# Attention with a windowed softmax and routed experts on one core: the order of the turned norm, queries, keys, values and exponentials between the two units of a tile

## The chip, the cores and the metric

One NeuronCore of one Trainium2 chip. The metric is the device time of one execution in microseconds; the program runs on one core.

## The reference

`x` is 8 sequences of 1024 positions of 128 features, in float32. The block computes

```python
x = x + attn(layernorm(x), Wq, Wk, Wv, Wo)      # 16 heads of 8, window of the last 64 positions
x = x + ffn(layernorm(x), w_router, w1, w2, bias)  # 8 experts, top 2 with a capacity, GELU
```

In `attn` the scores `q.k * 8**-0.5` of each position with the 64 positions up to itself go through a softmax and weigh the values; the heads, side by side, are multiplied by `Wo`. In `ffn` each position is sent to its two best experts (as far as they have room) and the results are added, weighted by the gates.

## The kernel before, in words

The attention part works in slots, one for each tile of 128 positions: 8 slots a sequence (t = 0 to 7), 64 in all, `slot(b, t)`. Each engine has its own `slot`, a list written out by hand, run in that order; semaphores tie the lists together. The chip's engines are TensorE (PE), VectorE (DVE), ScalarE (ACT), GpSimd (POOL) and SyncE (SP, which issues transfers).

A slot has two units, u = 2g and 2g + 1 for slot number g, for two groups of heads; each has its own two banks of `sT_ps`. For one unit:

- TensorE fills the banks with the window's mask and the scores (`fill`, lines 1108 to 1118). This is done a slot ahead.
- VectorE takes maxima over parts of them, turned (`part_max`, line 687, writes `kmax`).
- TensorE turns these again (`maxima_T`, line 1127, into `tail_ps` for first units and `o_ps` for second units).
- VectorE reduces them and prepares the shift (`shifts`, lines 693 to 701, writes `moving`).
- TensorE adds the shift to the scores (`shifted`, line 1135).
- ScalarE takes the exponential (`exps`, line 520, writes `probsT`).
- TensorE weighs the values with it (`weighted`, line 1143, into `u_ps`).

Once both units of a tile are weighted, ScalarE copies `u_ps` (`weighted_out`, line 525), TensorE turns it (`weighted_T`, line 1152, into `o_ps`), VectorE divides by the sums (`normalise`, lines 709 and 713), TensorE folds it (`context_T`, line 1158), ScalarE copies it (line 529), TensorE multiplies by `Wo` (`project`, line 1163), and VectorE adds `x` (`residual`, line 722). These steps run in the two following slots.

For each pair of tiles (n, numbered through all sequences) there is the preparation: ScalarE makes the normed rows (`normed`, line 473), TensorE turns them (`normed_T`, line 1086), ScalarE copies them (line 488); TensorE makes queries and keys (`query_key`, lines 1092 and 1093), ScalarE copies queries into a block form, four instructions (line 495), and keys, two (line 499); TensorE makes values (`values`, line 1098), ScalarE copies them in four instructions (line 510). All of it goes through one bank, `proj_ps`. The turned norm comes in even slots, queries and keys in odd ones, both in the first half of the slot (ahead of `shifted(2g + 1)`); values of the pair that begins in the next slot come in the second half of odd slots.

Other work sits at certain slots from the second sequence on: the second norm's rows of the sequence before are made by ScalarE in slot 4 (`normed_again`, line 482), turned by TensorE in slots 4 and 5 (line 1169, in `o_ps`) and copied by ScalarE in slot 5 (line 533); the router's matmuls stand in slots 5 and 6 (line 1193); VectorE's statistics, norm steps and routing are spread over all slots (`gap`, `small`). GpSimd sends routed rows and adds the bias, at counts of `s_scoresT`. After the attention part the experts run. VectorE's list is, for each slot: part maxima of unit 2g + 1, small work, `residual`, `shifts(2g + 1)`, part maxima of unit 2g + 2, small work, `normalise`, `shifts(2g + 2)`.

TensorE's list is that of the second `slot` printed below, ScalarE's the first; the lines of the diff are in them. A semaphore is waited for by count, as here in ScalarE's copy of queries (a pair's buffer is free when the scores of the pair before last are made):

```python
act.wait_ge(s_qk, n + 1)
if n >= 2:
    act.wait_ge(s_fill, 4 * n - 4)
```

Of the kernel before, what the change touches and what calls it, by code (L numbers as in the profile page):

```python
# [22 lines left out]
PAIRS = TILES // 2  # L23
# [25 lines left out]
def moe_block_kernel(nc, x, wq, wk, wv, wo, w_router, w1, w2, bias, out):  # L49
    ctx = ExitStack()  # L50
    with ctx:
# [410 lines left out]
        def _(act):  # L462
# [27 lines left out]
            def query_key(n, p, bank=proj_ps):  # L490
                act.wait_ge(s_qk, n + 1)
                if n >= 2:
                    act.wait_ge(s_fill, 4 * n - 4)
                for h in range(HQ):
                    nc.scalar.activation(qbd[:, p % 2, :, :, h, :].rearrange("p s b q -> p (s b) q"),  # L495
                                         bank[:, 0:2 * P].rearrange("p (c q) -> p c q", q=BLK), ACT.Copy,
                                         scale=quadmask[:, h:h + 1])
                for gp in range(2):
                    last = nc.scalar.activation(kT[:, gp, BLK + p * 2 * P:BLK + (p + 1) * 2 * P],
                                                bank[:, 2 * P:4 * P], ACT.Copy, scale=evenodd[:, gp:gp + 1])  # L500
                last.then_inc(s_k_sb, 1)
# [52 lines left out]
            def slot(b, t, first=False, last=False):  # L554
# [4 lines left out]
                if t == 7 and not first:  # L559
                    gate_exps(b - 1)  # L560
                if not (first and t == 0):
                    weighted_out(g - 1)
                if t % 2 == 0 and (t < 4 or not last):
                    normed_T(b * PAIRS + (t + 4) // 2, (t + 4) // 2 % PAIRS)
                if t % 2 == 1 and (t < 5 or not last):
                    query_key(b * PAIRS + (t + 3) // 2, (t + 3) // 2 % PAIRS)
# [4 lines left out]
                exps(g, 1)  # L571
                if t == 4 and not first:
                    normed_again(b, 1)
                if t % 2 == 1 and (t < 7 or not last):
                    values(b * PAIRS + (t + 1) // 2, (t + 1) // 2 % PAIRS)
                if t == 0 or t in (4, 6) and not last:
                    normed(b * PAIRS + (t + 6) // 2)
                if t == 3 and not last:
                    normed(b * PAIRS + 4)
# [6 lines left out]
            query_key(0, 0)  # L586
# [5 lines left out]
            query_key(1, 1, u_ps)  # L592
# [487 lines left out]
        def _(pe):  # L1080
# [126 lines left out]
            def slot(b, t, first=False, last=False):  # L1207
# [4 lines left out]
                shifted(2 * g)  # L1212
                if done:
                    pe.wait_ge(s_exp, 2 * g)
                    weighted((t - 1) % TILES, 1)
# [7 lines left out]
                if t % 2 == 1 and (t < 5 or not last):  # L1223
                    query_key(b * PAIRS + (t + 3) // 2, (t + 3) // 2 % PAIRS)
                if t % 2 == 0 and (t < 4 or not last):
                    n = b * PAIRS + (t + 4) // 2
                    pe.wait_ge(s_v_sb, n - 1)
                    pe.wait_ge(s_k_sb, n)
                    normed_T(n, (t + 4) // 2 % PAIRS)
# [3 lines left out]
                maxima_T(2 * g + 1)  # L1233
                pe.wait_ge(s_exp, 2 * g + 1)
                if ahead:
                    if t % 2 == 1:
                        pe.wait_ge(s_k_sb, b * PAIRS + (t + 1) // 2 + 1)
                    fill((t + 1) % TILES, 0)
                if t == 5 and not first:
# [19 lines left out]
                if t % 2 == 1 and (t < 7 or not last):  # L1259
                    n = b * PAIRS + (t + 1) // 2  # L1260
                    if t < 5 or not last:
                        pe.wait_ge(s_k_sb, n + 2)
                    values(n, (t + 1) // 2 % PAIRS)
# [143 lines left out]
```

## Time and profile before

| | |
|---|---|
| median of 3 runs | 861.02 us (860.0 to 861.64) |
| the profiled execution | 864.88 us, span 863.0 us |
| PE busy (matmuls) | 760.3 us, 88% of the span |
| PE weight loads | 544.6 us, 63% |
| DVE busy | 519.1 us, 60% |
| ACT busy | 451.1 us, 52% |
| POOL busy | 357.1 us, 41% |
| the exponentials (L520) | 128 of 1035 ns, 132.4 us |
| the part maxima (L687) | 128 of 1246 ns, 159.5 us |

The span is one profiled execution on the core. Busy times are sums over it; a matmul's end is modelled and matmuls are pipelined, so a busy PE isn't at its peak, and weight loads (PEld) overlap matmuls. In a row of the timeline the first number is the start in us from the span's start, the second the length; several like instructions are merged into one row (x8); in brackets stands how long the engine had been idle before and what ended that. L687 is line 687 of the kernel. The attention part fills some 555 us of the span, the experts the rest.

### The profile page before, as it was taken

The numbers are of one execution on the slowest core, as the hardware profiler recorded it, in microseconds if no ns is written. First come the engines' busy times: TensorE is split into PE (matmuls) and PEld (weight loads), VectorE is DVE, ScalarE is ACT, GpSimd is POOL, SyncE is SP. The second block draws the span as 40 slices with busy tenths as digits, with TensorE's granted clock in tenths as the row PEclk, the third lists the DMA queues.
The fourth block names the chain that finished last, engine by engine and source line by source line (L and its number), as shares of the span: only waits on it lengthen the run. The fifth ranks groups of instructions, "written<-read, shape, count | busy, mean of one in ns | idle before, by whom it ended". The sixth has DMA issues, their size and how long they took to land. (4 is left out here: it accounts for less than half of the span.)

```text
span 863.0 us, 19198 instructions
## 1 busy us (share of the span) xinstructions
PE 760.3 (88%) x7469; PEld 544.6 (63%) x7469; DVE 519.1 (60%) x1623; ACT 451.1 (52%) x923; POOL 357.1 (41%) x318
## 2 busy tenths in 40 slices
PE   7999999999999999999999998427999889889983
PEld 3556666666566566566666555314988778778872
DVE  7888888988888888887887887610222212211210
ACT  5576685585585585585586664202444334334421
POOL 3000000032232222322322343562877877877877
PEclk9999999999999999999999999557999999999997
DMA  4942000010110010010010011113364554554533
GB/s 137 387 160 62 8 15 8 34 33 25 50 33 21 31 47 30 22 56 30 21 57 30 21 66 40 67 51 117 32 111 59 93 101 58 96 97 59 87 31 33
DMA packets 50132, 54.21 MB, mean 63 GB/s; under 512 B 6018, under 2 KB 39449, under 8 KB 49025
## 3 DMA queue, kind: packets, MB, share of 16 engines
q0 software_dynamic: 22528, 17.22, 14.0%
q1 hardware_dynamic: 27520, 35.86, 12.6%
q8 instruction: 56, 0.92, 0.4%
q14 instruction: 28, 0.22, 0.1%
HBM read 17.70 MB, written 31.59 MB: 57 GB/s over the span
## 5 line engine op out<-in xcount | busy, mean ns | idle before, releaser
L445 POOL DMA_INDIRECT out<-y_sb,xg x128 | 199.2, 1556 | 71.1 <-issue 55.0
L363 POOL DMA_INDIRECT slots_dram<-send_rows,slot_id x112 | 110.3, 985 | 229.4 <-PE sT_ps L1135 163.1
L520 ACT ACTIVATE probsT<-sT_ps 128x1024 f32<-128x1024 f32 x128 | 132.4, 1035 | 60.2 <-PE sT_ps L1135 58.7
L687 DVE TRANSPOSE_TENSOR_REDUCE kmax<-sT_ps 128x32 f32<-128x1024 f32 x128 | 159.5, 1246 | 6.2 <-PE sT_ps L1118 5.7
L619 ACT ACTIVATE hT<-sT_ps 128x512 f32<-128x512 f32 x128 | 76.6, 599 | 154.7 <-PE sT_ps L1347 139.1
L1118 PE MATMUL sT_ps<-qbd,kT 64*128 64x256 f32 x1024 | 133.2, 380 | 0.0
L1347 PE MATMUL sT_ps<-xT_hl,w_hl 128*128 128x512 f32 x384 | 105.1, 426 | 24.8 <-DVE xT_hl L1045 18.5
L1055 DVE TENSOR_TENSOR y_sb<-o_ps,xg 128x256 f32<-128x256 f32 x32 | 13.6, 425 | 188.3 <-DMA out<-y_sb,xg 106.2
L1118 PEld LDWEIGHTS sT_ps<-qbd,kT 64*128 64x128 f32 x1024 | 98.6, 191 | 9.8
L1347 PEld LDWEIGHTS sT_ps<-xT_hl,w_hl 128*128 128x128 f32 x384 | 75.9, 204 | 43.9 <-DVE xT_hl L1045 19.1
L380 POOL TENSOR_TENSOR xbias<-x_sb,bias_sb 128x256 f32<-128x256 f32 x32 | 23.5, 734 | 192.8 <-PE sT_ps L1135 192.8
L1143 PE MATMUL u_ps<-probsT,v_sb 128*32 128x128 f32 x2048 | 82.9, 280 | 0.0
L1135 PE MATMUL sT_ps<-moving,ones 64*128 64x512 bf16 x256 | 49.9, 386 | 21.4 <-DVE moving L701 17.9
L1143 PEld LDWEIGHTS u_ps<-probsT,v_sb 128*32 128x32 f32 x2048 | 48.3, 109 | 29.6 <-issue 29.4
L1359 PE MATMUL o_ps<-w_sb,hT 128*128 128x128 f32 x512 | 62.7, 275 | 0.0
L1359 PE MATMUL proj_ps<-w_sb,hT 128*128 128x128 f32 x512 | 62.4, 275 | 0.0
L1359 PEld LDWEIGHTS o_ps<-w_sb,hT 128*128 128x128 f32 x512 | 59.8, 192 | 0.3 <-ACT hT L619 0.2
L1359 PEld LDWEIGHTS proj_ps<-w_sb,hT 128*128 128x128 f32 x512 | 59.7, 192 | 0.0
L701 DVE TENSOR_TENSOR moving<-negmax_hl,blocks 128x512 bf16<-128x512 bf16 x128 | 54.4, 425 | 4.4
L529 ACT COPY ctxT<-tail_ps 128x128 f32<-128x128 f32 x64 | 17.0, 266 | 72.6 <-PE tail_ps L1158 72.4
L495 ACT ACTIVATE qbd<-proj_ps,quadmask 128x256 f32<-128x256 f32 x124 | 48.7, 475 | 11.3 <-PE proj_ps L1093 9.8
L510 ACT ACTIVATE v_sb<-proj_ps 128x256 f32<-128x256 f32 (+1 forms) x124 | 37.2, 324 | 32.7 <-PE proj_ps L1098 31.9
(171 smaller groups left out, 1124.7 us busy)
## 6 DMA issues: line engine op xcount, KB each, us to landing
slots_dram<-empty_rows SPq DMA_DIRECT2D x8, 1096.0 KB, 16.7
xg<-slots_dram SPq DMA_DIRECT2D x32, 274.0 KB
out<-xbias SPq DMA_DIRECT2D x32, 128.0 KB
w_sb<-in_L_ffn_w SPq DMA_DIRECT2D x16, 256.0 KB
send_rows<-rows_sb SPq DMA_DIRECT2D x7, 548.0 KB, 3.2
out<-y_sb,xg POOLq DMA_INDIRECT x128
slots_dram<-send_rows,slot_id POOLq DMA_INDIRECT x112
out<-empty_rows SPq DMA_DIRECT2D x1, 1024.0 KB, 24.4
```

The costliest lines, as they stand in the source:

```text
L363: pool.indirect_dma_start(out=slots_dram, out_offset=bass.IndirectOffsetOnAxis(ap=slots[:, k, j:j + 1].bitcast(U32), axis=0), in_=rows[:, ...
L445: pool.indirect_dma_start(out=out, out_offset=bass.IndirectOffsetOnAxis(ap=xg[:, r, 4 * c + k, ROW - 1:ROW].bitcast(U32), axis=0), in_=y_s ...
L495: nc.scalar.activation(qbd[:, p % 2, :, :, h, :].rearrange("p s b q -> p (s b) q"), bank[:, 0:2 * P].rearrange("p (c q) -> p c q", q=BLK), ...
L520: nc.scalar.activation(probsT[:, gp].rearrange("p b k h q -> p (b k h q)"), sT_ps[:, gp].rearrange("p b c -> p (b c)"), ACT.Exp).then_inc( ...
L619: nc.scalar.activation(hT[:, c % 2, f, :], hidden_ps[f], ACT.Gelu_apprx_tanh).then_inc(f_gelu, 1)
L687: nc.vector.tensor_reduce(kmax[:, u % 2, :], sT_ps[:, u % 2].rearrange("p b (c q) -> p (b c) q", q=32), AX.X, ALU.max, apply_transpose=Tru ...
L701: nc.vector.tensor_tensor(out=moving[:, u % 2, :, :], in0=negmax_hl[:, :].unsqueeze(1).to_broadcast([P, 16, 32]), in1=blocks[:, :, :], op= ...
L1118: last = mm(sT_ps[:, gp, b, blk * 2 * P:(blk + 1) * 2 * P], kT[rows, gp, at:at + P], qbd[rows, t // 2 % 2, t % 2, blk, :, :].rearrange("p ...
L1135: last = mm(sT_ps[:, u % 2, b, :], ones[rows, :], moving[rows, u % 2, :, :].rearrange("p c q -> p (c q)"), start=False, stop=True, skip_gr ...
L1143: last = mm(u_ps[STRIP * c:STRIP * (c + 1), (2 * blk + gp) * P:(2 * blk + gp + 1) * P], v_sb[:, t // 2, 2 * (t % 2) + blk, 4 * b + 2 * gp ...
L1347: last = mm(hidden_ps[f], w1_hl[:, r, a, f * P:(f + 1) * P], xT_hl[:, c % 2, b, :], start=(i == 0), stop=(i == 2))
L1359: last = mm(y_ps[h][:, k % 2 * D:(k % 2 + 1) * D], hT[:, c % 2, f, k * P:(k + 1) * P], w2_sb[:, r, f, :], start=(f == 0), stop=(f == FC - 1))
```

## The change

On TensorE the turned norm goes from behind the projection to right behind the first unit's shift, and no longer waits for the copy of values. Queries and keys go behind the second unit's maxima instead of ahead of them. Values go from the second half of odd slots to the first half of even slots, behind the next tile's scores, for the pair that follows the one under way (in slot 0 for the pair of slots 2 and 3). Waits are placed accordingly: queries and keys wait for the copy of values of the pair n, values for the copy of the turned norm of the next pair.

On ScalarE the copy of the turned norm goes ahead of the output's copy; the copies of queries and keys are split, with the second unit's exponential between them; the copies of values follow that exponential in even slots. `normed` of slot 4 goes to slot 5. VectorE, GpSimd and SyncE are unchanged.

```diff
@@ -487,7 +487,7 @@
                 act.wait_ge(s_xnT, n + 1)
                 nc.scalar.copy(xnT[:, BLK + p * 2 * P:BLK + (p + 1) * 2 * P], bank[:, 0:2 * P]).then_inc(s_xnT_sb, 1)
 
-            def query_key(n, p, bank=proj_ps):
+            def queries(n, p, bank=proj_ps):
                 act.wait_ge(s_qk, n + 1)
                 if n >= 2:
                     act.wait_ge(s_fill, 4 * n - 4)
@@ -495,6 +495,8 @@
                     nc.scalar.activation(qbd[:, p % 2, :, :, h, :].rearrange("p s b q -> p (s b) q"),
                                          bank[:, 0:2 * P].rearrange("p (c q) -> p c q", q=BLK), ACT.Copy,
                                          scale=quadmask[:, h:h + 1])
+
+            def keys(n, p, bank=proj_ps):
                 for gp in range(2):
                     last = nc.scalar.activation(kT[:, gp, BLK + p * 2 * P:BLK + (p + 1) * 2 * P],
                                                 bank[:, 2 * P:4 * P], ACT.Copy, scale=evenodd[:, gp:gp + 1])
@@ -558,38 +560,40 @@
                 exps(g, 0)
                 if t == 7 and not first:
                     gate_exps(b - 1)
+                if t % 2 == 0 and (t < 4 or not last):
+                    normed_T(b * PAIRS + (t + 4) // 2, (t + 4) // 2 % PAIRS)
                 if not (first and t == 0):
                     weighted_out(g - 1)
-                if t % 2 == 0 and (t < 4 or not last):
-                    normed_T(b * PAIRS + (t + 4) // 2, (t + 4) // 2 % PAIRS)
                 if t % 2 == 1 and (t < 5 or not last):
-                    query_key(b * PAIRS + (t + 3) // 2, (t + 3) // 2 % PAIRS)
+                    queries(b * PAIRS + (t + 3) // 2, (t + 3) // 2 % PAIRS)
                 if t == 4 and not first:
                     normed_again(b, 0)
                 if t == 5 and not first:
                     normed_again_T(b, 1)
                 exps(g, 1)
+                if t % 2 == 1 and (t < 5 or not last):
+                    keys(b * PAIRS + (t + 3) // 2, (t + 3) // 2 % PAIRS)
+                if t % 2 == 0 and (t < 6 or not last):
+                    values(b * PAIRS + (t + 2) // 2, (t + 2) // 2 % PAIRS)
                 if t == 4 and not first:
                     normed_again(b, 1)
-                if t % 2 == 1 and (t < 7 or not last):
-                    values(b * PAIRS + (t + 1) // 2, (t + 1) // 2 % PAIRS)
-                if t == 0 or t in (4, 6) and not last:
+                if t == 0 or t in (3, 5, 6) and not last:
                     normed(b * PAIRS + (t + 6) // 2)
-                if t == 3 and not last:
-                    normed(b * PAIRS + 4)
                 if not (first and t == 0):
                     context_T(g - 1)
 
             normed(0)
             normed_T(0, 0)
             act.wait_ge(c_dve, 1)
-            query_key(0, 0)
+            queries(0, 0)
+            keys(0, 0)
             act.wait_ge(c_dve, 2)
             act.wait_ge(c_ones, 1)
             values(0, 0, o_ps)
             normed(1)
             normed_T(1, 1, u_ps)
-            query_key(1, 1, u_ps)
+            queries(1, 1, u_ps)
+            keys(1, 1, u_ps)
             normed(2)
             for t in range(TILES):
                 slot(0, t, first=True)
@@ -1210,6 +1214,10 @@
                 done, left = not (first and t == 0), not (first and t < 2)
 
                 shifted(2 * g)
+                if t % 2 == 0 and (t < 4 or not last):
+                    n = b * PAIRS + (t + 4) // 2
+                    pe.wait_ge(s_k_sb, n)
+                    normed_T(n, (t + 4) // 2 % PAIRS)
                 if done:
                     pe.wait_ge(s_exp, 2 * g)
                     weighted((t - 1) % TILES, 1)
@@ -1220,22 +1228,27 @@
                     if t == 1 and b > 1:
                         counts(b - 2).then_inc(s_pos, 1)
                     project(g - 2)
-                if t % 2 == 1 and (t < 5 or not last):
-                    query_key(b * PAIRS + (t + 3) // 2, (t + 3) // 2 % PAIRS)
-                if t % 2 == 0 and (t < 4 or not last):
-                    n = b * PAIRS + (t + 4) // 2
-                    pe.wait_ge(s_v_sb, n - 1)
-                    pe.wait_ge(s_k_sb, n)
-                    normed_T(n, (t + 4) // 2 % PAIRS)
 
                 if t == 5 and not first:
                     pe.wait_ge(s_xn2T_sb, 2 * (b - 1) + 1)
                 maxima_T(2 * g + 1)
+                if t % 2 == 1 and (t < 5 or not last):
+                    n = b * PAIRS + (t + 3) // 2
+                    pe.wait_ge(s_v_sb, n)
+                    query_key(n, (t + 3) // 2 % PAIRS)
+
                 pe.wait_ge(s_exp, 2 * g + 1)
                 if ahead:
                     if t % 2 == 1:
                         pe.wait_ge(s_k_sb, b * PAIRS + (t + 1) // 2 + 1)
                     fill((t + 1) % TILES, 0)
+                if t % 2 == 0 and (t < 6 or not last):
+                    n = b * PAIRS + (t + 2) // 2
+                    if t < 4 or not last:
+                        pe.wait_ge(s_xnT_sb, n + 2)
+                    else:
+                        pe.wait_ge(s_k_sb, n + 1)
+                    values(n, (t + 2) // 2 % PAIRS)
                 if t == 5 and not first:
                     pe.wait_ge(s_negmax, 2 * g + 2)
                     normed_again_T(b, 1)
@@ -1256,11 +1269,6 @@
                     counts(b - 1, proj_ps).then_inc(s_pos, 1)
                 if ahead:
                     maxima_T(2 * g + 2)
-                if t % 2 == 1 and (t < 7 or not last):
-                    n = b * PAIRS + (t + 1) // 2
-                    if t < 5 or not last:
-                        pe.wait_ge(s_k_sb, n + 2)
-                    values(n, (t + 1) // 2 % PAIRS)
                 if ahead:
                     pe.wait_ge(s_exp, 2 * g + 2)
                     fill((t + 1) % TILES, 1)
```

## Rows read from the trace of the kernel before

**Rows 1.** The page's busy time by engine, whole span

```profile
PE 760.3 (88%) x7469; PEld 544.6 (63%) x7469; DVE 519.1 (60%) x1623; ACT 451.1 (52%) x923; POOL 357.1 (41%) x318
```

**Rows 2.** Windows: one sequence; us, then busy of PE, PEld, DVE, ACT, POOL

```profile
269.28:334.60 65.32, 62.30 (x735) 40.25 (x733) 55.87 (x178) 44.14 (x95) 18.67 (x20) 1.00 0.10 35
```

**Rows 3.** Waits of VectorE (DVE), 62 to 520 us: total, times, longest

```profile
DVE negmax L693 <- PE o_ps L1127: 17.0, 32, 1.0
DVE x_sb L722 <- PE tail_ps L1163: 15.7, 17, 2.3
DVE rden L709 <- PE o_ps L1152: 11.2, 19, 0.8
```

**Rows 4.** Waits of TensorE's matmuls (PE), the same stretch

```profile
PE sT_ps L1135 <- DVE moving L701: 13.2, 53, 0.7
```

**Rows 5.** Timeline, sequence 0, tile 5 and into tile 6: start, length

```profile
58.90 0.39 PE L1135 MATMUL sT_ps<-moving,ones 64*128 64x512 bf16 x2
...
59.79 0.30 PEld L1163 LDWEIGHTS tail_ps<-wo_sb,ctxT 128*128 128x128 f32 x2 [0.20 <-issue]
...
60.01 0.30 PEld L1092 LDWEIGHTS proj_ps<-xnT,wq_sb 128*128 128x128 f32 x2
...
61.07 0.16 PEld L1127 LDWEIGHTS o_ps<-ident,kmax 128*32 128x32 f32 x8 [0.33 <-issue]
...
61.43 0.10 PEld L1112 LDWEIGHTS sT_ps<-onehot,window 64*128 64x128 bf16 x2 [0.20 <-issue]
...
61.57 0.29 DVE L693 TENSOR_REDUCE negmax<-o_ps 128x32 f32<-128x128 f32 x1 [0.96 <-PE o_ps L1127]
...
62.88 0.39 PE L1135 MATMUL sT_ps<-moving,ones 64*128 64x512 bf16 x2 [0.19 <-DVE moving L701]
...
64.46 0.26 DVE L709 RECIPROCAL rden<-o_ps 128x16 f32<-128x16 f32 x1 [0.48 <-PE o_ps L1152]
64.71 0.52 PEld L1098 LDWEIGHTS proj_ps<-wv_sb,xnT 128*128 128x128 f32 x4 [0.20 <-issue]
...
65.36 0.39 PE L1112 MATMUL sT_ps<-onehot,window 64*128 64x512 bf16 x2
...
65.38 0.29 DVE L693 TENSOR_REDUCE negmax<-tail_ps 128x32 f32<-128x128 f32 x1
65.46 1.22 ACT L510 ACTIVATE v_sb<-proj_ps 128x256 f32<-128x256 f32 x4 [1.06 <-PE proj_ps L1098]
...
66.54 0.66 PE L1158 MATMUL tail_ps<-fold,ctx_sb 128*128 128x64 f32 x4
...
67.13 0.39 PE L1135 MATMUL sT_ps<-moving,ones 64*128 64x512 bf16 x2
```

**Rows 6.** Timeline, the rest of tile 6

```profile
68.66 0.43 PE L1127 MATMUL o_ps<-ident,kmax 128*32 128x128 f32 x8
...
70.46 0.39 PE L1135 MATMUL sT_ps<-moving,ones 64*128 64x512 bf16 x2 [0.19 <-DVE moving L701]
```

**Rows 7.** Timeline, sequence 4, tiles 4, 5 and 6

```profile
315.46 1.63 ACT L482 ACTIVATE rows_sb<-x_sb,ln,rs_y 128x128 f32<-128x128 f32 x4
...
318.17 0.39 PE L1135 MATMUL sT_ps<-moving,ones 64*128 64x512 bf16 x2
318.27 0.59 ACT L533 COPY xn2T<-o_ps 128x512 f32<-128x512 f32 x1 [0.18 <-PE o_ps L1169]
...
327.62 0.39 PE L1135 MATMUL sT_ps<-moving,ones 64*128 64x512 bf16 x2
...
329.94 0.29 DVE L722 TENSOR_TENSOR x_sb<-tail_ps,x_sb 128x128 f32<-128x128 f32 x1 [2.06 <-PE tail_ps L1163]
```

**Rows 8.** Timeline, sequence 5, tile 0

```profile
344.15 0.39 PE L1135 MATMUL sT_ps<-moving,ones 64*128 64x512 bf16 x2
...
347.49 0.39 PE L1135 MATMUL sT_ps<-moving,ones 64*128 64x512 bf16 x2 [0.19 <-DVE moving L701]
```

**Rows 9.** Timeline, sequence 5, tile 2

```profile
363.77 1.25 DVE L687 TRANSPOSE_TENSOR_REDUCE kmax<-sT_ps 128x32 f32<-128x1024 f32 x1 [0.56 <-PE sT_ps L1118]
```
## The prediction, made before the changed kernel was run

> **What bounds the kernel now.** I read the page first. TensorE's matmuls are busy 88% of the span, VectorE 60%, ScalarE 52% [rows 1]. The change touches only the attention part, eight sequences of eight slots (a slot is one tile of 128 positions, and has two units of scores), so I took the windows of one sequence next: of 65.32 us the matmuls are busy 62.30, weight loads 40.25, VectorE 55.87, ScalarE 44.14 [rows 2]. Then who waits for whom: VectorE waits 17.0 us for the maxima in `o_ps` (second units only), 15.7 for the projected output, 11.2 for the turned output [rows 3]; TensorE waits 13.2 us for `moving` [rows 4]. Both wait for each other, so neither is "the" bound; the order of the work decides, and it must be walked in the timeline.
>
> A light slot pair shows the walk (sequence 0, slots 5 and 6, [rows 5, 6]). I call S0 and S1 the starts of the matmul that adds the shift of the first and second unit (L1135). S0 to S1 is 58.90 to 62.88, 3.98 us; S1 to the next S0 (67.13) 4.25; in the even slot 3.33 (to 70.46). In the odd slot's first half queries and keys stand ahead of the maxima, VectorE waits 0.96 us for them, and starts `negmax` at 61.57, from which 1.31 us later S1 can go. In its second half VectorE waits 0.48 for the turned output, but S0 at 67.13 comes 1.75 us after `negmax` at 65.38, not 1.31: TensorE is still busy with values (L1098), the scores (L1112 to 66.54) and the context. So an odd slot is held by TensorE's order twice, an even one by the loop through VectorE.
>
> **The change, step by step.** All costs are from start to start. Shift and weighted sum 0.89 (58.90 to 59.79); projection 0.22; queries and keys 1.06 (60.01 to 61.07); maxima 0.36 (to 61.43); values 0.65 (64.71 to 65.36); scores 1.18 (65.36 to 66.54); context 0.59 (to 67.13) [rows 5]. The turned norm is what the even slot's path to the maxima has more: 68.66 less 67.13 is 1.53, less 0.89 and 0.22, so 0.42 [rows 5, 6]. Nothing is added or taken away; the number of instructions stays on each engine, no DMA is touched, and SP's and POOL's queues keep their order (what they wait for shifts only with the rest).
>
> Odd slot, first half: the maxima go ahead of queries and keys. They can start at S0 + 1.15 (the part maxima of VectorE end about then), so `negmax` starts some 0.9 us earlier. That doesn't buy 0.9: queries and keys now stand between the maxima and the scores of the next tile, which end S1's queue at 1.15 + 0.36 + 1.06 + 1.18 = 3.75. Saved: 3.98 - 3.75 = 0.23 in a light pair. Second half: values are gone, the queue is 0.89 + 0.59 + 0.36 + 1.18 + 0.59 = 3.61, under the loop through VectorE, 62.88 to 64.46 to 65.38 plus 1.31 = 3.81. Saved: 4.25 - 3.81 = 0.44. Even slot, first half: values come between the scores and S1: 1.53 + 0.36 + 1.18 + 0.65 = 3.72 against 3.33, lost 0.39. Even second half: 3.81 before and after. A light pair gains 0.23 + 0.44 - 0.39 = 0.28 us. Slots 1 of sequence 0 to 2 of sequence 1, ten slots, are light: **-1.4 us**.
>
> Later sequences have VectorE's norm and routing work between the units, so they gain less. I carried the same costs through one sequence from slot 7 to slot 7, each start being the later of its queue and its input; VectorE's own work between two steps stays as long as it is. Slot 0 as the example: it is entered 0.24 us early, and its S0 0.49 early, as values no longer hold TensorE in slot 7. S0 to S1, 344.15 to 347.49 or 3.34 [rows 8], becomes 3.72: S1 at 343.66 + 3.72 = 347.38 for 347.49. The loop of 3.81 follows, so slot 1 is entered 0.10 early: slot 0 has lost 0.14. Slot 7 loses 0.05 in the same way. Slot 2 gains 0.32, since S0 no longer waits behind slot 1's values and VectorE waits there for scores (0.56 us before 363.77, [rows 9]). Slots 3 and 5 lose 0.05 and 0.07, slot 4 gains 0.05. Slots 5 to 6 need care: S0 to S0 is 318.17 to 327.62, 9.45 us [rows 7], all of it TensorE's queue (the steps above come to 3.71 and 4.26, and 1.48 go to four normed rows turned and half a router), and it loses the values' 0.65. But in slot 6 VectorE waits 2.06 us for the projected output (329.94, [rows 7]), and now the turned norm stands ahead of that: 0.42 back. Net 0.12 gained in slot 6. The sum is -0.18 us a sequence, over some 6.6 such sequences: **-1.2 us**.
>
> ScalarE: each exponential of an odd slot's second unit passes the two key copies. It starts 0.43 us after S1, which queries mostly let it do already, so this is worth nothing by itself, and the keys are used two slots later; if that cover were gone it would cost their 0.9 us. In even slots the copy of the turned norm (0.39) goes ahead of the output's copy, which is wanted only at S1 + 0.9: nothing. In slot 4 the values' 1.22 us [rows 5] now stand ahead of four normalisations of 1.63 [rows 7], with one `normed` of 0.86 moved to slot 5 in exchange. The copy of the turned rows (318.27, [rows 7]) comes some 0.4 us later, to 319.0; the maxima, which wait for it in slot 5, are ready to start at about 319.0 as well. Bounds: nothing to 0.4 us a sequence; I take nothing, as their start would move only by the excess. New waits on TensorE (keys of the pair ahead of the turned norm, values' copy ahead of queries, the norm's copy ahead of values) end on work that is over a microsecond old by then: nothing, or if a copy slipped, up to its 0.4.
>
> The one price that no row shows is that of values between scores and a shift. From the context's row, which is as many matmuls in the same place, it is 0.59; with the issue gap of 0.33 that follows queries and keys (61.07, [rows 5]) on top it is 0.65 + 0.33 = 0.98. I take 0.65, its cost where it stands now.
>
> **Sum.** -1.4 - 1.2 = -2.6 us, I take -2.7 with some 0.1 from the last sequence, which makes no values ahead. The profiled execution, 864.88 us for a span of 863.0, would become 862.2; it lies 3.9 above the median of the runs, 861.02, from which the forecast is 858.3. What this kernel's measurement can tell from no change is 0.2%, 1.7 us.
>
> **A rule against this sum.** The rows put both engines at the limit by turns. The Trainium skill (Perfetto Trace Analysis, Identifying the Most-Contended Engine) says that matmul busy time is a poor measure of TensorE and that weight loads should be taken, with occupancy for VectorE. By it TensorE stands at 40.25 of 65.32 us, VectorE at 55.87 [rows 2], and VectorE would be what bounds. That gives the first rival.
>
> **Rivals.** (1) VectorE bounds, and its waits for the maxima turn into time: up to 17.0 us off [rows 3], 844.0. Against it: behind `negmax` at 61.57 VectorE needs the scores issued at 61.43, which end just as it is done with the shift, and queries and keys still stand ahead of them. Chance 0.07. (2) Nothing moves: the heavy sequences give 0 instead of 0.18 and light ones half, as VectorE's own work fills the slots: -0.7, 860.3. For it: in some 57 slots only 32 second units made VectorE wait [rows 3]. Chance 0.25. (3) Slower: values after the scores hold S1 in even slots, hence weighted sum, turned output and reciprocal, for which VectorE waits there already (11.2 us, [rows 3]). With 0.98 for 0.65 the light pair ends at -0.28 + 0.33 = +0.05, and in a heavy sequence slots 0, 4 and 6 pay 0.33 each: -0.18 + 0.99 = +0.8, times 6.6 is +5.3: 866.4. It decides from about 0.28 us above the values' 0.65. Chance 0.13. The forecast keeps 0.55.
>
> The forecast's own bounds: a heavy sequence could give all of the odd halves' and slot 5's saving, some -0.9, so -7 us in all, 854; or nothing with the price half way, 861. Towards the rivals I go to 863.0 and leave out the rest of (3) and all of (1). Faster by over 0.2%: the forecast and (1), less its upper edge, 0.60; within: 0.26; slower: 0.14.
>
> **What would show it.** Sequence 0, slots 5 and 6: odd S0 to S1 about 3.75, then 3.81; even 3.72, then 3.81, 15.1 a pair for 15.38. `negmax` on `o_ps` no longer waits in odd slots, but `kmax` then waits for scores. S0 to S0 across slot 5 about 8.9, with a wait of about 2 us for the projected output still in slot 6. A sequence takes 65.1 us. If S0 to S1 in even slots is over 4.0, rival 3 is true; if a sequence takes under 64, the loops do not stand as I have them.

## The result: slower by 0.6%, and the profile after

The changed kernel takes 866.39 us (864.96 to 867.31, 6 runs) against 861.59 (860.0 to 862.56, 6 runs): 1.0062 of the kernel before, 95% interval 1.0043 to 1.0081. Its profiled execution took 866.43 us, span 864.2. 858.3 was forecast.

The page's busy times stay within 4 us of where they were [rows 1], but for TensorE, whose matmuls are busy 12 us longer and whose weight loads 5:

```profile
PE 772.1 (89%) x7469; PEld 549.7 (64%) x7469; DVE 515.8 (60%) x1623; ACT 449.0 (52%) x923; POOL 356.3 (41%) x318
```

The window of one sequence, cut like [rows 2], is 65.46 us where 65.32 stood and 65.1 was forecast; matmuls fill 63.66 of it, not 62.30:

```profile
270.12:335.58 65.46, 63.66 (x736) 40.84 (x734) 55.36 (x177) 43.93 (x97) 18.62 (x20) 1.00 0.11 35
```

VectorE's waits, 62 to 520 us, and TensorE's below, answer to [rows 3, 4]; the last line is from the kernel before, which those rows don't show:

```profile
DVE kmax L691 <- PE sT_ps L1122: 21.2, 30, 1.0
DVE x_sb L726 <- PE tail_ps L1167: 15.6, 17, 2.5
DVE rden L713 <- PE o_ps L1156: 15.2, 24, 0.9
...
PE sT_ps L1139 <- DVE moving L705: 6.8, 23, 0.3
```
```profile
DVE kmax L687 <- PE sT_ps L1118: 4.3, 8, 1.0
```

The 17.0 us for the maxima are gone. The waits of `kmax`, the part maxima, for scores went from 4.3 us to 21.2, those for the turned output rose by 4.0. TensorE waits half as long for VectorE. The change turned an order in which the two waited for each other into one held more by TensorE's queue. Lines after the diff stand 4 lower: L691 is L687 of before.

The light pair (TensorE, sequence 0, slots 5 and 6, start and length) answers to [rows 5, 6]:

```profile
59.33 0.39 PE L1139 MATMUL sT_ps<-moving,ones 64*128 64x512 bf16 x2
...
60.23 0.49 PE L1167 MATMUL tail_ps<-wo_sb,ctxT 128*128 128x128 f32 x2
60.64 0.43 PE L1131 MATMUL o_ps<-ident,kmax 128*32 128x128 f32 x8
61.00 0.70 PE L1096 MATMUL proj_ps<-xnT,wq_sb 128*128 128x256 f32 x2
...
62.06 0.39 PE L1116 MATMUL sT_ps<-onehot,window 64*128 64x512 bf16 x2
...
63.15 0.38 PE L1139 MATMUL sT_ps<-moving,ones 64*128 64x512 bf16 x2
...
66.95 0.39 PE L1139 MATMUL sT_ps<-moving,ones 64*128 64x512 bf16 x2
67.27 0.44 PE L1090 MATMUL proj_ps<-ident,xn 128*128 128x128 f32 x2
67.64 0.64 PE L1147 MATMUL u_ps<-probsT,v_sb 128*32 128x128 f32 x16
...
68.22 0.49 PE L1167 MATMUL tail_ps<-wo_sb,ctxT 128*128 128x128 f32 x2
68.63 0.43 PE L1131 MATMUL o_ps<-ident,kmax 128*32 128x128 f32 x8
68.99 0.39 PE L1116 MATMUL sT_ps<-onehot,window 64*128 64x512 bf16 x2
...
70.17 0.71 PE L1102 MATMUL proj_ps<-wv_sb,xnT 128*128 128x128 f32 x4
70.82 0.39 PE L1139 MATMUL sT_ps<-moving,ones 64*128 64x512 bf16 x2
```

From start to start of the shifts (L1139), as in the prediction, it is 3.82 us, then 3.80, 3.87 and 3.81 (the next one at 74.63): 15.30 us a pair, for 15.38 before and 15.09 forecast (3.75, 3.81, 3.72, 3.81). Three of the forecast's costs can be read off. Values between scores and a shift cost 70.17 to 70.82, 0.65, as taken. From the projection to the maxima it is 60.23 to 60.64, 0.41, where 0.22 was taken. With the turned norm ahead of the weighted sum, S0 to the maxima is 66.95 to 68.63, 1.68, where 1.53 was taken. The last step of it is again the projection ahead of the maxima, 68.22 to 68.63, 0.41.

The two profiled executions hardly differ: a span of 864.2 us against 863.0. From the first start of `negmax` on `tail_ps` to the last it is 514.67 us against 513.43. In both the granted clock fell in some slots 6: twice in the changed kernel (10.84 and 10.83 us for 9.34, together 3.0) and once in the kernel before (10.94 for 9.62, 1.3). Without these slots' excess the two stretches are 511.7 and 512.1 us, so the profile shows 0.4 us won by the order and not the 4.8 lost in the medians. The kernel before's profiled execution was itself 3.9 above its median.

### The profile page after: what moved, and what is told of

The parts are those of the page before. It is cut to its first block and busy times, and to the rows that moved or that the text cites. A ratio compares the mean times of both kernels' runs of the same rounds, so it can differ in the third digit from the quotient of the medians.

```text
span 864.2 us, 19228 instructions
## 1 busy us (share of the span) xinstructions
PE 772.1 (89%) x7469; PEld 549.7 (64%) x7469; DVE 515.8 (60%) x1623; ACT 449.0 (52%) x923; POOL 356.3 (41%) x318
## 5 line engine op out<-in xcount | busy, mean ns | idle before, releaser
L363 POOL DMA_INDIRECT slots_dram<-send_rows,slot_id x112 | 110.4, 986 | 233.3 <-PE sT_ps L1139 167.7
L691 DVE TRANSPOSE_TENSOR_REDUCE kmax<-sT_ps 128x32 f32<-128x1024 f32 x128 | 159.3, 1244 | 22.7 <-PE sT_ps L1122 22.6
L1139 PE MATMUL sT_ps<-moving,ones 64*128 64x512 bf16 x256 | 49.9, 386 | 13.5 <-DVE moving L705 10.4
L1162 PEld LDWEIGHTS tail_ps<-fold,ctx_sb 128*128 128x128 f32 x256 | 34.2, 194 | 24.2 <-DVE negmax L697 22.0
```

Of the source, the lines that this page charges most:

```text
L363: pool.indirect_dma_start(out=slots_dram, out_offset=bass.IndirectOffsetOnAxis(ap=slots[:, k, j:j + 1].bitcast(U32), axis=0), in_=rows[:, ...
L691: nc.vector.tensor_reduce(kmax[:, u % 2, :], sT_ps[:, u % 2].rearrange("p b (c q) -> p (b c) q", q=32), AX.X, ALU.max, apply_transpose=Tru ...
L1139: last = mm(sT_ps[:, u % 2, b, :], ones[rows, :], moving[rows, u % 2, :, :].rearrange("p c q -> p (c q)"), start=False, stop=True, skip_gr ...
```

## Experiments

I cut the change into its parts on either kernel, then took GpSimd's indirect sends of routed rows (L363) away. Each ratio is to the kernel before, run in turns with it on the same chip; four chips, A to D, were used. A slot's time, in tables and text, is from one start of `negmax` on `tail_ps` (L693, L697) to the next. The expectations weigh theories against each other: O, later called L, is that TensorE's order costs more than I took; V, that values between scores and shift do; C, that the granted clock differs; G, that VectorE stands behind GpSimd's sends.

### One part at a time, chip A

`r0_before`, the kernel before again, is the control. 

> The kernel before, unchanged, for more profiles and clocks. Theory O (the order costs more on TensorE than I priced: the maxima 0.42 us behind the projection where I took 0.22, the turned norm 0.37 behind the shift): a sequence takes 65.3 us but for stretches at the lower clock; time 861.6. Theory C (the granted clock is what differs): the mean clock of its runs lies at 0.950 or above, against 0.942 to 0.946 of the changed kernel, and each fall in the attention part costs some 1.3 us, as in the one slot of 10.94 us for 9.62.

863.86 us, 0.9991 (0.9979 to 1.0003); profiled span 860.7, no slot 6 prolonged. The mean granted clock of its runs is 0.950.

`v1_norm_back`: the changed kernel with the turned norm and its copy in their old places.

```diff
 shifted(2 * g)
-if t % 2 == 0 and (t < 4 or not last):
-    pe.wait_ge(s_k_sb, n)
-    normed_T(n, (t + 4) // 2 % PAIRS)
...
 project(g - 2)
+if t % 2 == 0 and (t < 4 or not last):
+    pe.wait_ge(s_k_sb, n)
+    normed_T(n, (t + 4) // 2 % PAIRS)
```

> The changed kernel with the turned norm and its copy back in their old places. Theory O: even first halves 3.72 us for 3.87, in slot 6 the projected output 0.4 us earlier, so a heavy sequence some 0.6 us shorter and the whole about 861.7 for 866.4. Theory C: 866 if the clock stays at 0.944, 861 to 862 if it goes back to 0.950, with the slots away from the falls unchanged. Theory V (values between the scores and the shift are the cost): no gain, 866.

862.38 us, 0.9967 (0.9954 to 0.998): faster than the kernel before. The early norm is what turns the change from a gain into a loss. A heavy sequence takes 65.13 us here, 0.33 less than in the changed kernel's profile, where some 0.6 less was expected; the mean granted clock of its runs is 0.950.

`v3_maxima_first`: the kernel before with only `query_key` moved behind `maxima_T(2 * g + 1)`. 

> The kernel before with only the second units' maxima ahead of queries and keys on TensorE. Theory O: odd first halves 3.82 us for 3.98 in light slots, VectorE then waits for scores in place of maxima; heavy sequences as before; 860.8, within 0.2% of before. Theory C: no difference if the clock is that of before.

866.95 us, 1.0012 (0.9996 to 1.0029): no change clear of the noise. Slot 5 is 8.84 us for 8.37; with the keys' copy split off it is 8.57 (y6, below).

`v4_norm_early`: the kernel before with only the turned norm moved ahead of `weighted`, and its copy ahead of `weighted_out`. 

> The kernel before with only the turned norm right behind the first unit's shift on TensorE, and its copy ahead of the output's on ScalarE. Theory O: the maxima of even slots 0.15 us later and the projected output 0.37 later, which slot 6 pays in full: 0.7 to 0.9 us a sequence, 866 to 868. Theory V: 861.6, as values stay. Theory C: 861.6 with the clock of before.

879.32 us, 1.0164 (1.0146 to 1.0183). The early norm alone costs 14 us, which no theory of mine had. The profiled execution, 886.13 us, was the slowest of the six. Its slot 2 in sequences 3 to 7 took 8.9 to 10.5 us for 8.4 before. VectorE, in slot 2 of sequence 3, and below it GpSimd at the same time:

```profile
238.15 0.29 DVE L693 TENSOR_REDUCE negmax<-o_ps 128x32 f32<-128x128 f32 x1 [1.50 <-remote]
...
235.41 0.98 POOL L363 DMA_INDIRECT slots_dram<-send_rows,slot_id  x1 [3.05 <-PE sT_ps L1135]
236.69 0.98 POOL L363 DMA_INDIRECT slots_dram<-send_rows,slot_id  x1 [0.30 <-issue]
```

`negmax` had its data from about 236.3 (TensorE's maxima start at 235.89, 0.43 long) and VectorE was free from 236.65. It starts at 238.15, 0.48 after the second send's end at 237.67. In sequences 5 to 7 the wait is 1.03 to 1.14 us and ends 0.17 to 0.20 before the send does.

### The other parts and the clock, chip B

`a0_after`, the changed kernel again. 

> The changed kernel unchanged, again, for another profile and the clocks of its runs. Theory C: its mean clock stays near 0.945, the attention part again shows falls in slots 6, some 1.5 us each, and with them comes most of the 0.6% over before; without its falls the attention part is 0.9 us shorter than before's. Theory O: the loss is there in slots at the full clock.

872.37 us, 1.0067 (1.0045 to 1.009). This profile, span 870.4, has the stall too. Slot 2 of sequences 3 to 7 takes 9.33, 9.32, 8.63, 8.59 and 8.57 us, where the first profile of the same kernel had 7.68 to 7.89. The window of sequence 4 is 67.08 us (for the 65.46 above):

```profile
270.67:337.75 67.08, 63.81 (x736) 40.84 (x733) 55.83 (x177) 44.12 (x97) 18.64 (x20) 1.00 0.11 35
```

`v2_values_keys`: only the values moved, and the keys' copy split off; queries and keys ahead of the maxima and the turned norm behind the projection as before. 

> The kernel before with values in even first halves and the keys' copy behind the exponential, but with queries and keys ahead of the maxima and the turned norm behind the projection, as before. Theory O (the maxima right behind the projection put the scores 0.2 us later in odd slots): heavy sequences 64.7 us or less against 65.15 of the version with the maxima first, light pairs 15.3 against 15.15; 859 to 861 beside 862.4 of that version on the last chip, and 864.9 of before. Theory V: slower than before.

863.86 us, 0.9951 (0.9934 to 0.9967). The values' move, with the keys' copy split off, is what is good in the change, and the version beats both kernels.

`x5_keys_back`: the changed kernel with the keys' copies ahead of the exponential again. 

> The changed kernel with the keys' copies ahead of the second unit's exponential again. If the split is needed once queries and keys come later on TensorE: the exponential of odd slots starts 0.9 us later, the next scores wait for it, some 0.6 us an odd slot, 15 us and more in all, 880. If it is worth nothing by itself, as I had it: 866.

875.0 us, 1.0082 (1.0057 to 1.0107), 2.6 us above the changed kernel there and within its interval. By the slots the split is worth something once the maxima come first: slot 5 took 8.84 for 8.56 in sequences 1 to 6. Slot 2 stalls as in `a0_after` (9.33, 9.32, 8.62, 8.59, 8.59).

`x6_filler`: one 128x512 matmul of zeros ahead of the turned norm in slot 6, to keep TensorE busy.

```diff
 pe.wait_ge(s_k_sb, n)
+if t == 6:
+    mm(proj_ps[:, :], zeros[:, 0:P], zeros[:, :], start=True, stop=True)
 normed_T(n, (t + 4) // 2 % PAIRS)
```

It tests whether the loss comes from drops of the granted clock: in the first profile slot 6 took 10.84 instead of 9.34 in two sequences. 

> The changed kernel with one matmul of zeros, 128x512 in bf16, ahead of the turned norm in slots 6. It adds 0.2 us to the path of slot 6, 1.5 us in all. Theory C, if the falls in slot 6 come from how little TensorE does there: they go, mean clock 0.949 or more, and the time falls by 1 to 2 us. Otherwise: 1.5 us slower than the changed kernel, with the same falls.

874.2 us, 1.0073 (1.0047 to 1.01). Its profile has no slot 6 prolonged from a fallen clock, where `a0_after` has one (10.83), but each slot 6 takes 9.52 for 9.34 by the filler, 1.3 us in all, which would eat up what one drop less gives back. So this run by itself decides nothing. The clocks on record say more. In three series of the changed order (`a0_after`, z1, `a1_after`, on chips B, C and D) the mean granted clock of the runs is 0.9477, 0.9474 and 0.9482, and of the kernel before's runs beside them 0.9479, 0.9478 and 0.9482. As an estimate from the z1 windows at the end of this text, one prolonged slot takes 0.002 off a mean (0.43 of 4 us in 864.7). The clocks then differ by at most a fifth of such a slot, some 0.3 us. On these chips the drops are not what makes the changed kernel slower. In the first measurement its runs had 0.945, and the kernel before has a clock on record for its profiled execution only, 0.951.

### Without GpSimd's sends, chips C and D

The 96 sends inside the slots are left out, each replaced by an increment of another semaphore, so that their rows never reach the experts:

```diff
 if turn == (t, half) and t >= 3:
-    send_tile(send_rows, n // 2, n % 2)
+    pool.sem_inc(s_skip, 1)
```

`y3_before_nosend`: 

> The kernel before, with GpSimd's 96 indirect sends of routed rows inside the attention slots left out (each replaced by a semaphore increment; the 32 sends behind the attention stay), so those rows never reach their experts. Theory G (VectorE stands behind GpSimd's sends): slots in which VectorE's step met a send shorten a little, attention from the first slot to the last 503.2 goes to about 500 to 502, ratio to the kernel before 0.995 to 0.998. Theory L (only TensorE's order costs): the same attention time within 0.5 us, ratio 0.999 to 1.001.

859.21 us, 0.9977 (0.9957 to 0.9998): 2.0 us by the ratio.

`y4_after_nosend`: 

> The changed kernel with the same 96 sends left out. Theory G: slot 2 of sequences 3 to 7, which took 9.33, 9.32, 8.63, 8.59 and 8.57 us in the changed kernel's last profile, goes to 7.7 to 7.9 in all of them, the attention becomes some 6 us shorter, and the ratio to the kernel before is 0.996 to 0.999. Theory L (the order on TensorE alone makes it slower): slot 2 keeps its 8.6 to 9.3 us, the ratio stays at 1.005 to 1.008, and stands as far above that of the kernel before without sends as the two stood with them.

860.25 us, 0.9988 (0.9969 to 1.0007). The two are 0.11% apart, not 0.6%, each with an interval of about 0.2% to either side; the runs of this one had the higher granted clock, 0.950 for 0.949 in the mean.

`z1_after_sends_moved`: the changed kernel, all its sends kept, one of slot 2's pair a slot earlier.

```diff
-following = [(0, 0), (0, 1), (1, 0), (1, 1), (2, 0), (2, 0)]
+following = [(0, 0), (0, 1), (1, 0), (1, 1), (1, 1), (2, 0)]
```

> The changed kernel, nothing left out, with one of the two sends that GpSimd issues back to back in slot 2's first half moved to slot 1's second half. Theory G: VectorE's step in slot 2 no longer meets the end of the second send, slot 2 goes to 7.7 to 8.0 us (slot 1 may pay up to 0.5 instead), ratio to the kernel before 0.999 to 1.003. Theory L: nothing changes, 1.005 to 1.008.

866.06 us, 1.0057 (1.0039 to 1.0075). A miss: slot 2 is at 7.88 to 8.11 in its profile, with no stall, and the time is not regained. Three slots 6 of its profile are prolonged (10.78 and 10.80 us for 9.34, and 10.08 for 8.97 in the last sequence).

`z2_v2_sends_moved`: 

> The version with only the values and the keys' copy moved (0.9951 to the kernel before), with the same send moved from slot 2 to slot 1. Theory G: slot 2 took 8.15 there with no long stall, so there is little to win: 0.993 to 0.996. Theory L: 0.995, unchanged.

858.18 us, 0.9959 (0.9937 to 0.9981): nothing won over 0.9951.

`a1_after`, the changed kernel on chip D: 

> Control, the changed kernel on this chip: ratio to the kernel before 1.004 to 1.008. If its profile shows slot 2 of sequences 3 to 7 at 8.5 us or more, the ratio should lie at 1.006 or above; at 7.7 to 7.9, below.

865.24 us, 1.0034 (1.0012 to 1.0056), slot 2 at 7.68 to 7.90 in its profile.

`y5_v4_nosend`: 

> The kernel before with the turned norm alone moved early (1.0164 of the kernel before with all its sends), without the 96 sends inside the slots. Theory G (VectorE stands behind sends whose place in the step the early norm has shifted): slot 2, which took 8.9 to 10.5 us, goes to 8.1 or less, and the ratio falls to 0.998 to 1.003. Theory L (the norm's place costs on TensorE): it stays at 1.012 or more.

867.12 us, 1.0059 (1.0035 to 1.0082), for 1.0164 with the sends. Its slot 2 is down to 7.77 to 7.90. Some 9 of the early norm's 14 us went with the sends; 7 remain over the kernel before without its own (1.0059 less 0.9977, measured on two chips). The slots agree: from the first start of `negmax` to the last it is 514.08 us against y3's 508.21, 5.9 more. It fits neither theory's range; both have a share.

`y7_after_skip_early` (only the 30 sends of slots 0 to 2 left out): 

> The changed kernel without the 30 sends of slots 0 to 2 of sequences 3 to 7; the 66 of slots 3 to 7 stay. If slots 0 to 2 carry the loss (their VectorE steps are the ones that stood in the profiles): ratio 0.999 to 1.002. If the loss is spread over all sends by number: 1.004 to 1.005.

862.61 us, 1.0007 (0.9983 to 1.003).

`y8_after_skip_late` (only the 66 of slots 3 to 7): 

> The changed kernel without the 66 sends of slots 3 to 7; the 30 of slots 0 to 2 stay. If slots 0 to 2 carry the loss: 1.004 to 1.007. If it is spread by number: 1.001 to 1.002.

861.93 us, 1.0014 (0.998 to 1.0049). Beside `a1_after`'s 1.0034 either group seems to bring 2 us or so, but the three intervals overlap: which sends count isn't settled.

`y6_v1_nosend`: 

> Values, maxima and keys moved, turned norm left behind the projection, without the 96 sends inside the slots. By slots: no stall in slot 2, a sequence of 65.0 us (65.14 with sends). If sends cost every order alike (2.5 us, as in the kernel before): ratio 0.9935 to 0.9945. If they cost only where a step falls behind one, which this order's slots hardly showed: 0.9955 to 0.9965.

857.42 us, 0.9896 (0.9877 to 0.9915), below both ranges. The kernel before took 866.47 there, in the earlier series on the same chip 861.31, so the last two ratios carry more doubt than their intervals say.

`y9_v2_nosend`: 

> Values and keys alone moved, without the 96 sends. By slots: a sequence of 64.2 to 64.5 us (64.64 with sends, the kernel before without sends 64.8). Alike for every order: ratio 0.992 to 0.993; only where a step falls behind a send: 0.9935 to 0.995. In either case below y6 by 0.1 to 0.2%, which is the price of the maxima ahead of queries and keys.

860.58 us, 0.9944 (0.9922 to 0.9966), in the range of the second case, but not below y6. By runs it stands above y6, by slots below. Its runs had granted clocks of 0.939 to 0.943, those of y6 0.947 to 0.953, and its profile has a prolonged slot 6 in sequence 1 (10.68 us for 9.11), so these two can't be ranked by their times. I go by the slots.

### What the slots say when no send disturbs them

The windows of sequence 4, `negmax` of slot 7 to `negmax` of slot 7, one line from each profile, in the order before (y3), values and keys (y9), maxima as well (y6), the whole change (y4), and the early norm alone (y5):

```profile
267.32:332.11 64.79, 62.40 (x737) 40.43 (x734) 55.56 (x177) 44.14 (x95) 2.93 (x4) 1.00 0.06 19
```
```profile
270.37:334.64 64.27, 62.39 (x737) 40.42 (x735) 55.33 (x177) 44.24 (x97) 2.94 (x4) 1.00 0.06 19
```
```profile
268.23:333.04 64.81, 62.98 (x737) 40.72 (x735) 55.14 (x178) 43.86 (x97) 2.94 (x4) 1.00 0.06 19
```
```profile
268.36:333.68 65.32, 63.64 (x737) 40.83 (x735) 55.10 (x177) 43.81 (x97) 2.92 (x4) 1.00 0.06 18
```
```profile
270.39:335.98 65.59, 63.04 (x737) 40.55 (x735) 55.81 (x178) 44.11 (x95) 2.94 (x4) 1.00 0.05 18
```

The same by slot, us, sequence 4:

| | 0 | 1 | 2 | 3 | 4 | 5 | 6 | 7 | sum |
|---|---|---|---|---|---|---|---|---|---|
| before, no sends (y3) | 7.47 | 8.13 | 7.91 | 7.79 | 7.59 | 8.36 | 9.62 | 7.92 | 64.79 |
| values, keys (y9) | 7.53 | 8.13 | 7.89 | 7.80 | 7.52 | 8.37 | 9.11 | 7.92 | 64.27 |
| + maxima (y6) | 7.53 | 8.25 | 7.89 | 7.89 | 7.53 | 8.57 | 9.11 | 8.04 | 64.81 |
| + early norm (y4) | 7.68 | 8.25 | 7.89 | 7.89 | 7.68 | 8.56 | 9.34 | 8.03 | 65.32 |
| change, sends (first profile) | 7.68 | 8.30 | 7.89 | 7.93 | 7.68 | 8.56 | 9.34 | 8.08 | 65.46 |
| before, sends | 7.39 | 8.13 | 8.43 | 7.79 | 7.59 | 8.37 | 9.62 | 8.00 | 65.32 |

Values and keys bring 0.52 a sequence, nearly all in slot 6. The maxima first take 0.54, in slots 1, 3, 5 and 7. The early norm takes 0.51, in slots 0, 4 and 6 (alone, 0.80). The change is +0.53 a sequence by TensorE's order. Over the whole attention, the first slot's `negmax` to the last one's, it is 508.21 (y3) to 510.83 (y4), +2.6 us; the runs' medians differ by 1.0.

With the sends in place and no stall the balance is another: +0.14 in sequence 4 (the last two rows), since the kernel before has slot 2 at 8.43 and the changed one at 7.89.

### What a send does to VectorE

The same kernel in two profiles, slot 2 of sequence 4. First `a1_after`, VectorE and then GpSimd:

```profile
300.72 0.27 DVE L726 TENSOR_TENSOR x_sb<-tail_ps,x_sb 128x128 f32<-128x128 f32 x1
300.91 0.28 DVE L697 TENSOR_REDUCE negmax<-o_ps 128x32 f32<-128x128 f32 x1
...
300.75 0.98 POOL L363 DMA_INDIRECT slots_dram<-send_rows,slot_id  x1 [0.30 <-issue]
```

Then `a0_after`, with TensorE's maxima and next shift below:

```profile
298.65 0.29 DVE L726 TENSOR_TENSOR x_sb<-tail_ps,x_sb 128x128 f32<-128x128 f32 x1
300.17 0.29 DVE L697 TENSOR_REDUCE negmax<-o_ps 128x32 f32<-128x128 f32 x1 [1.22 <-remote]
...
298.60 0.98 POOL L363 DMA_INDIRECT slots_dram<-send_rows,slot_id  x1 [0.30 <-issue]
...
297.80 0.43 PE L1131 MATMUL o_ps<-ident,kmax 128*32 128x128 f32 x8
301.48 0.39 PE L1139 MATMUL sT_ps<-moving,ones 64*128 64x512 bf16 x2 [1.43 <-DVE moving L705]
```

In the one the residual's add starts 0.03 us before the second send of the pair and `negmax` follows after 0.19 us. In the other it starts 0.05 us after the send, and `negmax`, whose maxima are ready at about 298.2, starts 1.52 us later, 0.59 after the send's end at 299.58; TensorE then waits 1.43 us for `moving`. In all five sequences of `a0_after` the add starts 0.04 to 0.06 after the send, in none of the ten slots 2 of the first profile and `a1_after` does it. `x5_keys_back` and `x6_filler` show the same stall with the same 0.05 to 0.06. In sequences 5 to 7 of these three `negmax` waits only 0.50 to 0.53 us and starts some 0.1 before the send ends, so for this wait the fixed time after the end holds in sequences 3 and 4 alone. In the kernel before (`r0_before`) the add starts 0.31 us ahead of the send in sequences 3 and 4, and `negmax` is under way before the send:

```profile
295.25 0.27 DVE L722 TENSOR_TENSOR x_sb<-tail_ps,x_sb 128x128 f32<-128x128 f32 x1
295.44 0.28 DVE L693 TENSOR_REDUCE negmax<-o_ps 128x32 f32<-128x128 f32 x1
...
295.56 0.98 POOL L363 DMA_INDIRECT slots_dram<-send_rows,slot_id  x1 [0.30 <-issue]
```

There `kmax` pays, more mildly: its 0.56 us in [rows 9] ends at 363.77, 0.54 after a send that began at 362.25 and lasted 0.98, and without sends slot 2 is 7.91, not 8.43. So the kernel before pays 0.5 us to the sends in sequence 4 (0.7 and 0.8 in 5 and 6), the changed kernel 0.14 where it doesn't stall and 1.8 where it does (1.2 in 5 and 6); between the two lie 0.08 us in the start of the add against the send.

## Why the prediction was wrong

The direction was wrong, and the miss has two parts. Steps of the sum, forecast at -2.6 us, come to +2.6 where no send disturbs them and to -0.4 in the first profile with its prolonged slots set aside. And there is a cost, that of the sends, that the sum didn't have.

**"They can start at S0 + 1.15" (maxima first).** They start at S0 + 1.31. The step kept the 0.22 that the projection took ahead of queries and keys [rows 5]; ahead of the maxima it takes 0.41. A cost from start to start belongs to a pair of neighbours, and the move changed the neighbour. The queue came to 1.31 + 0.36 + 1.06 + 1.09 = 3.82 instead of 3.75; the scores' 1.09 for 1.18 gave more than half of that back. In the heavy sequences the same move costs 0.54, where the walk had losses of 0.05 to 0.07 in slots 3, 5 and 7 and none in 1. `kmax` waits 0.98 us in slot 5 for the scores that queries and keys hold back. The wait of VectorE for the maxima that made the move look good was harmless: TensorE's queue had to be passed anyway. The first rival, at 844.0, is refuted: the 17.0 us of waits did vanish, and 21.2 us for scores came in their place. The Trainium skill (Perfetto Trace Analysis, Identifying the Most-Contended Engine) would judge TensorE by its weight loads. They are 40.84 of 65.46 us here, and TensorE seems far from its limit; the trace doesn't bear that out, since with VectorE's waits for the maxima gone the sequence is no shorter and the matmuls fill 63.66.

**"0.42 back" in slot 6 (turned norm early).** Nothing came back: with values and keys moved, slot 6 is 9.11 with the norm behind the projection and 9.34 with it early, so it costs 0.23 there. The slot as a whole goes from 9.62 to 9.34, better than the 0.12 forecast, but by the values' move, which has it at 9.11. The early norm also costs 0.15 each in slots 0 and 4, which the walk had at nothing beyond the values' price: 1.68 for 1.53 to the maxima. It is the same mistake as above. With the norm gone from between them the projection stands right ahead of the maxima and takes 0.41 there too, where 0.22 was kept, while the norm itself takes 0.37 in its new place for 0.42. Alone the early norm costs 0.80 a sequence.

**Slot 2 "gains 0.32", as "VectorE waits there for scores (0.56 us)" [rows 9].** The row names the scores, and I took its word. The wait ends 0.54 us after a send's end, and it vanishes without sends while no value has moved (7.91). So the gain was right by luck. Slot 2 went from 8.43 to 7.89, its part maxima no longer waiting; without sends there is nothing to gain (7.91 to 7.89). The heavy sum of -0.18 stood on it; without it that sum is +0.14. With sends, the first profile has +0.14 too, because slot 2 gave 0.22 and slot 6 0.16 more than forecast, and slots 0, 1, 3, 4, 5 and 7 lost 0.70 more.

**Held.** The values' 0.65 between scores and a shift (0.65 measured, so the third rival's 0.98 is refuted although its 866.4 us is near the result); the second halves at 3.80 and 3.81 for 3.81; slot 6's wait for the projected output (1.90 us at 330.93). The keys' split cost nothing; without it, by x5, slot 5 loses 0.28 and the whole 2.6 us within the noise. I had nothing.

**"SP's and POOL's queues keep their order (what they wait for shifts only with the rest)."** True of the order, wrong of the cost: where VectorE's step falls against a send decides over 1.4 us of slot 2 (9.33 for 7.89). By the runs the changed kernel is 1.0 us above the kernel before when neither has sends (chip C), and 2.9 to 5.8 when both have (1.0034 on D, 1.0067 on B). By that most of the loss is what the sends cost this order more than the old one. On B the stalls in the profile, 5.6 us in five slots 2, are as large as the loss. The difference on D, 0.34%, and the one without sends, 0.11%, aren't apart by more than their intervals.

**Open.** Where the 4.8 us of the first measurement are. The stall in slot 2 is shown in `v4_norm_early` and in the three profiles from chip B that have the early norm (`a0_after`, x5, x6), and absent from the first profile, `a1_after` and z1, whose runs are 1.0062, 1.0034 and 1.0057. By the slots of these three profiles the changed order loses less to the sends than the old one: from the first start of `negmax` to the last, prolonged slots set aside, the kernel before goes from 508.2 to 512.1 us with sends, the changed one from 510.8 to 511.7 in the first profile and to 518.7 with the stall. What makes the first profile longer than the one of before is the clock in slot 6. Some executions may stall and others not, or the time is lost in another way, and for the first measurement the clock isn't excluded; one profile of each series can't tell these apart. What is shown is the mis-sized steps, the stall where a profile has it, and that the early norm decides: without it the change is 0.9967 of the kernel before (chip A), with it 1.0034 to 1.0067 (the others).

## What to carry to other kernels

Cost a moved step by its new neighbours, not by the row of its old place, and take an engine's wait as worth something only where the other engine's queue behind it also gets shorter. Ask of each wait in a trace whether something on a third engine stands beside it: here VectorE's waits of 0.5 to 1.5 us, named after TensorE or nobody, lay over a GpSimd send and were gone without it. Test a bundle of moves one by one: here values and keys together were worth 0.5%, and the maxima and the norm took it back and more. The values' move with the keys' copy split off (0.9951) is the version to keep. And compare a profile's span with the median of the runs before explaining the one by the other.

## Unexpected behaviour of the hardware

In sequences 3 and 4 VectorE's reduction of a PSUM operand stood with its data ready until 0.48 to 0.59 us after a GpSimd indirect send's end. This happened where VectorE's add before it began 0.05 us after the send (`a0_after`) and also where the add had ended 0.04 before the send (`v4_norm_early`). Where the add began 0.03 us before the send and ran into it (`a1_after`), the reduction started on time, 0.16 us into the send. I have no rule that covers these three. The Trainium skill (SBUF — State Buffer, Who interferes with whom) has the two engines block each other over a shared pair of ports, by whichever issues first, and says that `tensor_reduce` never contends on trn2. The rows fit neither simply: the reduction came after the send's start in all three cases and waited in only two, and there it did wait, 1.22 and 1.50 us. Its own length stays at 0.28 to 0.29 us; what moves is its start. The measurement decides; whether the ports are the reason, no run here tells.

The granted clock falls now and then in slot 6, with TensorE's matmuls busy throughout. Windows of 4 us in `z1_after_sends_moved`, slot 6 of sequence 3, and the second window's part of the slot in sequence 4:

```profile
260.00:264.00 4.00, 4.00 (x45) 3.02 (x41) 2.48 (x7) 2.44 (x6) 0.98 (x1) 1.00 0.06 20
264.00:268.00 4.00, 4.00 (x26) 2.44 (x25) 2.46 (x9) 0.02 (x1) 0.00 (x0) 0.57 0.05 18
...
331.10:335.10 4.00, 3.99 (x48) 2.61 (x47) 3.29 (x11) 0.94 (x2) 0.15 (x1) 1.00 0.05 18
```

0.57 is a window mostly at the lower of the two levels, 1.2 GHz; about half as many matmuls issue (26 for 48), and that slot took 10.78 us instead of 9.34. Profiles with sends show none to three such slots; of the five without, only y9 has one, in sequence 1. That is too few to call it an effect.
